# Softmax sums moved from a second exponential to accumulating DMAs and a product with ones, with one-term scores for the maxima and a new order of work

## The reference

```
h = layernorm(x)                                   # over the 512 features, eps 1e-6
shift, scale, gate = split(silu(cond) @ mod_w + mod_b, 3)     # per batch
h = h * (scale + 1) + shift
q, k, v = split(h @ w_qkv)                         # 16 heads of 32 features
q = rope(layernorm(q) * q_norm_w); k = rope(layernorm(k) * k_norm_w)
scores = q @ k.T / sqrt(32)                        # per head, 512 x 512
o = softmax(scores) @ v
out = x + (o @ w_out) * gate
```

## Time and profile before

| what | us |
|---|---|
| runs: median (lowest to highest) | 1943.38 (1943.3 to 1945.53) |
| profiled execution, its own time | 1946.49 |
| span of the profiled execution | 1944.7 |
| TensorE busy | 1776.7 |
| VectorE busy | 1485.0 |
| ScalarE busy | 1487.2 |
| GpSimd busy | 434.4 |

### The profile page before, as it was taken

The page is one execution under the profiler, slowest core; times in us unless marked ns, Lnnn a source line. Parts: engine busy times, 40 slices in busy tenths (PEclk is TensorE's granted clock), DMA queues, the critical chain, the costliest instruction groups (busy, mean ns, idle before and its releaser), DMA issues.

```text
span 1944.7 us, 35999 instructions
## 1 busy us (share of the span) xinstructions
PE 1776.7 (91%) x13346; PEld 1030.4 (53%) x13346; DVE 1485.0 (76%) x2430; ACT 1487.2 (76%) x3145; POOL 434.4 (22%) x452
## 2 busy tenths in 40 slices
PE   4768899999999999999999999999999999997777
PEld 1645555555555555555555555555555555554333
DVE  6677778888888788878887888788878888875443
ACT  2248888888888888888888888888888888887663
POOL 0331222122212221222122212221222122221000
PEclk8879999999999999999999999999999999998769
DMA  5000010100101111010101010010111002000001
GB/s 193 27 6 28 6 44 23 50 28 17 55 28 50 34 39 34 23 55 17 55 28 50 23 49 29 18 55 28 50 33 40 28 17 63 16 28 22 21 18 66
DMA packets 35950, 72.77 MB, mean 37 GB/s; under 512 B 4513, under 2 KB 4513, under 8 KB 35778
## 3 DMA queue, kind: packets, MB, share of 16 engines
q1 hardware_dynamic: 35778, 70.47, 11.3%
HBM read 53.58 MB, written 16.88 MB: 36 GB/s over the span
## 4 chain that ended last, share of the span: by engine, by line
PE 80%; ACT 9%; issue 5%; DVE 5%; DMA 1%; ACTq 0%; SPq 0%; DVEq 0%
PE Y L261 26%; PE SM L370 13%; PE SA L397 10%; PE O L415 10%; PE Y L268 10%; ACT SM L527 4%; PE SA L401 3%; PE O L352 3%; PE SA L252 2%; ACT vals L504 2%; PE SA L379 2%; DVE qk_lo L676 1%; DVE qk_hi L674 1%; ACT probs L542 1%; ACT oT L519 1%
## 5 line engine op out<-in xcount | busy, mean ns | idle before, releaser
L527 ACT ACTIVATE SM<-SM,negmax 128x512 f32<-128x512 f32 x512 | 338.7, 664 | 130.8 <-DVE negmax L683 130.8
L683 DVE TENSOR_REDUCE negmax<-SM 128x2 f32<-128x1024 f32 x256 | 313.6, 1225 | 162.6 <-PE MB L370 155.9
L851 POOL TENSOR_TENSOR pair_part<-rows,rope_pair 128x256 f32<-128x256 f32 x128 | 94.5, 739 | 1312.8 <-DVE rows L660 1307.7
L527 ACT ACTIVATE MB<-MB,negmax 128x512 f32<-128x512 f32 x512 | 341.9, 671 | 0.0
L542 ACT ACTIVATE probs<-SM 128x1024 f32<-128x1024 f32 x256 | 262.8, 1027 | 72.0 <-PE SM L401 54.6
L683 DVE TENSOR_REDUCE negmax<-MB 128x2 f32<-128x1024 f32 x256 | 310.9, 1215 | 0.0
L261 PE MATMUL Y<-wqkv_hi,hT_hi 128*128 128x512 f32 x728 | 307.4, 422 | 0.3 <-ACT rows L493 0.3
L261 PE MATMUL Y<-wqkv_hi,hT_lo 128*128 128x512 f32 x728 | 306.7, 421 | 0.0
L415 PE MATMUL O<-probs,vals 128*32 128x512 f32 x2048 | 283.8, 627 | 5.9 <-ACT probs L543 5.9
L261 PE MATMUL Y<-wqkv_lo,hT_hi 128*128 128x512 f32 x728 | 289.2, 397 | 0.0
L543 ACT ACTIVATE probs<-SA 128x1024 f32<-128x1024 f32 x256 | 260.8, 1019 | 0.0
(11 more groups left out here) (140 smaller groups left out, 4108.6 us busy)
## 6 DMA issues: line engine op xcount, KB each, us to landing
xin<-in_x_dram SPq DMA_DIRECT2D x64, 256.0 KB, 2.9
xres<-in_x_dram SPq DMA_DIRECT2D x60, 256.0 KB, 2.6
out_dram<-xres SPq DMA_DIRECT2D x60, 256.0 KB, 2.0
shift_scale<-mod_rows SPq DMA_DIRECT2D x16, 512.0 KB, 4.2
gate<-mod_rows SPq DMA_DIRECT2D x16, 256.0 KB, 4.7
rows<-in_L_cond_mod_w_dram SPq DMA_DIRECT2D x1, 3072.0 KB, 10.0
probs<-in_L_cond_w_qkv_dram SPq DMA_DIRECT2D x2, 1024.0 KB, 12.7
vals<-in_L_cond_w_qkv_dram SPq DMA_DIRECT2D x1, 1024.0 KB, 15.6
```

Source lines behind the costliest of these rows:

```text
L527: ins = act.activation(qm_bank(i), qm_bank(i), ACT.Exp, bias=negmax[:, g % 2, t, i:i + 1], accum_out=sums[:, g % 2, t, i:i + 1])
L683: dve.tensor_reduce(negmax[:, g % 2, t, 2 * half:2 * half + 2], bank[:], AX.X, ALU.max, negate=True).then_inc(max_out, 1)
L851: pool.tensor_tensor(pair_part[:].rearrange("p h (i two) -> p h i two", two=2), swapped, rope_pair[:, t, j, :].rearrange("p (i two) -> p i ...
```

## The change

- **Scores by query** keep only the hi*hi term; they now serve only to find maxima. The maxima, negated, go straight into `cst`, without a logarithm; the low part that `cst` held is gone.
- **Key exponentials** therefore give unnormalized probabilities, three buffers of them. Their sum over a group's four key blocks is made by GpSimd-issued accumulating DMAs (`add_keys`): block 1 is added onto block 0's buffer, then 2, then 3, each 128 x 2048 float32. A float32 product with ones (`add_over_keys`) sums that buffer over its 128 partitions and spreads it over each head's 32 rows. ScalarE takes the logarithm and the exponential of its negative (`log_sums`, `inverse_sums`), and VectorE multiplies the finished oT by it (`scale_o`). For the last group only blocks 1 and 2 are added by DMA; the product with ones takes two buffers.
- **qk high parts** move from VectorE to ScalarE (`high_qk`); q and k are transposed into MB instead of O, one group ahead instead of two, with two ring buffers instead of three. Squares are taken from SBUF after the copy (`square`).
- **Roots** are guessed by ScalarE (exp(-ln/2), `guess_roots`) with one Newton step: 4 VectorE instructions instead of 11.
- **Order**: a quarter on TensorE is scores by key, values, scores by query, then one whole projection of 12 matmuls; high terms first. v is projected for tile s+4, q for s+6, k for s+5 or s+6; the output projection is of tile s-5. `xin` has two buffers instead of three.
- **Start**: weights come in pieces, w_q first; the modulation runs as four products side by side in four column groups, whose parts are added by a selection product. Batch 0's shift and scale come from that product directly, without DRAM. The first four tiles' statistics and roots are made together; the low parts of w_q and w_v are made by GpSimd; five tiles and their q, k, v products are ordered by hand before the loop.

The core of the diff:

```diff
@@ scores by query
-                for a, c in ((qk_hi, qk_hi), (qk_hi, qk_lo), (qk_lo, qk_hi)):
-                    for i in range(HG):
-                        r = head_rows(i)
-                        mm = pe.matmul(qm_bank(i), a[r, ring, 0, cols], c[r, ring, 1, :],
-                                       start=(a is qk_hi and c is qk_hi), stop=(a is qk_lo))
+                for i in range(HG):
+                    r = head_rows(i)
+                    mm = pe.matmul(qm_bank(i), qk_hi[r, g % 2, 0, cols], qk_hi[r, g % 2, 1, :], start=True, stop=True)
@@ TensorE, new
+            def add_over_keys(g, bank, buffers):
+                for m, a in enumerate(buffers):
+                    for i in range(HG):
+                        mm = pe.matmul(bank[head_rows(i), :], ones_r[:, 0:E].bitcast(F32), probs[:, a, i, :],
+                                       start=(m == 0), stop=(m == len(buffers) - 1), skip_group_check=True)
+                mm.then_inc(ones_done, 1)
@@ TensorE, one step
+            for s in range(LAST + 1):
+                transpose_c(s)
+                if group(s + 1):
+                    transpose_qk(s + 1, 0)
+                    transpose_qk(s + 1, 1)
+                scores_by_key(s, 0)
+                if s > 0:
+                    weigh_values(s - 1, 3)
+                if group(s + 1):
+                    scores_by_query(s + 1, 0)
...
+                    project(s + 4, 2, Y[:])
+
+                scores_by_key(s, 1)
+                if s > 0:
+                    pe.wait_ge(third_added, 16 * s)
...
+                    add_over_keys(s - 1, MB[:, 0, :], (sum_buffer(s - 1),))
+                weigh_values(s, 0)
+                if group(s + 1):
+                    scores_by_query(s + 1, 1)
...
+                    project_out(n, Y[:], 0, 4)
+                if tile(s + 6):
+                    transpose_x(s + 6)
+                if n >= 0:
+                    project_out(n, Y[:], 4, 12)
+
+                scores_by_key(s, 2)
+                weigh_values(s, 1)
+                if group(s + 1):
+                    scores_by_query(s + 1, 2)
...
+                    project(s + 6, 0, Y[:])
...
+                scores_by_key(s, 3)
+                weigh_values(s, 2)
+                if group(s + 1):
+                    scores_by_query(s + 1, 3)
+                if tile(s + 6):
+                    pe.wait_ge(raw_out, raw_count(s + 6, 0))
+                    project(s + 6, 1, Y[:])
@@ ScalarE
-            def query_exponentials(g, t, half):
...
+            def high_qk(g, j):
...
+                act.activation(qk_hi[:, g % 2, j, :], MB[:, j, :], ACT.Copy).then_inc(qk_high, 1)
+            def log_sums(g, bank):
...
+                act.activation(sum_inv[:], bank, ACT.Ln).then_inc(sum_ln, 1)
+            def inverse_sums(g):
+                act.wait_ge(sum_ln, g + 1)
+                act.activation(sum_inv[:], sum_inv[:], ACT.Exp, scale=-1.0).then_inc(sum_ready, 1)
+                    if t == 0:
+                        if g > 0:
+                            act.wait_ge(pv_step, n - 1)
+                            act.wait_ge(second_added, 16 * g)
...
+                    elif t == 1 and g > 0:
+                        act.wait_ge(pv_step, n - 1)
+                        act.wait_ge(third_added, 16 * g)
...
+                    elif t == 3:
+                        act.wait_ge(pv_step, n - 1)
+                        act.wait_ge(first_added, 16 * (g + 1))
@@ VectorE
+            def scale_o(g):
+                o = oT[:, (g // NG) % 2, g % NG, :]
+                dve.wait_ge(sum_ready, g + 1)
+                dve.wait_ge(o_out, g + 1)
+                dve.tensor_tensor(o, o, sum_inv[:], ALU.mult).then_inc(o_scaled, 1)
@@ GpSimd
+            def add_keys(g, t):
+                pool.wait_ge(s_exp, 2 * (TT * g + t) + 2)
+                if t == 1:
+                    pool.wait_ge(pv_step, TT * g + 1)
+                else:
+                    pool.wait_ge((first_added, second_added)[t - 2], 16 * (g + 1))
+                pool.dma_start(probs[:, sum_buffer(g)].rearrange("p h n -> p (h n)"),
+                               probs[:, probs_buffer(g, t)].rearrange("p h n -> p (h n)"), accum_op=ALU.add
+                               ).then_inc((first_added, second_added, third_added)[t - 1], 16)
+            for s in range(LAST + 1):
+                add_keys(s, 1)
+                if s - 5 >= 0:
+                    add_residual(s - 5)
+                if tile(s + 5):
+                    rotate(s + 5, 0)
+                add_keys(s, 2)
+                if tile(s + 5):
+                    rotate(s + 5, 1)
+                if s < LAST:
+                    add_keys(s, 3)
@@ start, SyncE
+            load_weight(0)
+            load_modulation(1)
+            load_modulation(0)
...
+            load_weight(2)
+            load_weight(1)
+            load_modulation(2)
```

More of the change, by code:

```diff
@@ L270, in project_out, with project_last @@
                     mm.then_inc(y_done, 1)
-            def project_last(t, bank, first, last):
+            def project_last(t, first, last):
+                bank = last_banks[t]
                 for g in range(first, last):
-                    for o, w in ((last_hi, wout_hi), (last_hi, wout_lo), (last_lo, wout_hi)):
-                        mm = pe.matmul(bank, o[:, g, t * P:(t + 1) * P], w[:, g, :],
-                                       start=(g == 0 and o is last_hi and w is wout_hi),
-                                       stop=(g == NG - 1 and o is last_lo))
+                    for i, (o, w) in enumerate(((last_hi, wout_hi), (last_hi, wout_lo), (last_lo, wout_hi))):
+                        mm = pe.matmul(bank, o[g][:, t * P:(t + 1) * P], w[:, g, :],
+                                       start=(g == 0 and i == 0), stop=(g == NG - 1 and i == 2))
@@ L461, in _, with modulation_parts @@
-            weigh_values(LAST, TT - 1)
-            pe.wait_ge(s_exp, 2 * TT * NS)
-            project_last(3, last_banks[3], 0, 3)
+            def modulation_parts(j, bank):
+                pe.wait_ge(ld_mod[j], 16)
+                for c in range(DT):
+                    mm = pe.matmul(bank[head_rows(c), :], siluT[:, c, :], modw_raw[j][:, c, :],
+                                   start=True, stop=True, skip_group_check=True)
+                mm.then_inc(mod_partial, 1)
+            pe.wait_ge(siluT_ready, 1)
@@ new lines, in _ @@
+            modulation_parts(1, SM[:, 1, :])
+            modulation_parts(0, SM[:, 0, :])
+            pe.wait_ge(sel_step, 4)
+            for j in (1, 0):
+                pe.wait_ge(parts_out, 2 - j)
+                pe.matmul(MB[:, j, :], sel_first, parts_sb[:, j, :], start=True, stop=True).then_inc(mod_first, 1)
+            for j in (1, 0):
+                pe.matmul(SM[0:NB, j, :], sel, parts_sb[:, j, :], start=True, stop=True).then_inc(mod_product, 1)
+            transpose_x(0)
+            project(0, 0, Y[:])
@@ new lines, in _ @@
+            pe.wait_ge(parts_out, 3)
+            pe.matmul(O[0:NB, :], sel, parts_sb[:, 2, :], start=True, stop=True).then_inc(mod_product, 1)
+            transpose_qk(0, 0)
+            transpose_qk(0, 1)
+            pe.wait_ge(raw_out, raw_count(4, 0))
+            project(4, 1, Y[:])
+            scores_by_query(0, 0)
+            transpose_x(5)
+            pe.wait_ge(raw_out, raw_count(4, 1))
+            project(5, 0, Y[:])
+            scores_by_query(0, 1)
+            pe.wait_ge(raw_out, raw_count(5, 0))
@@ L594, in _ @@
             dve.tensor_tensor(silu_sb, silu_sb, cond_sb, ALU.mult).then_inc(silu_ready, 1)
[L595 to L599 removed]
+            for c in range(1, DT):
+                if c > 1:
+                    dve.wait_ge(sel_step, c - 1)
+                dve.tensor_tensor(sel, ident[:, 0:NB] if c == 1 else sel, ident[:, E * c:E * c + NB], ALU.add
+                                  ).then_inc(sel_step, 1)
@@ new lines, in _ @@
+            weight_mean(0)
+            weight_centre(0)
+            modulation_sum(0, 1, SM[:, 1, :])
+            modulation_sum(1, 0, SM[:, 0, :])
+            for n in range(TT):
+                first_statistics(n)
+            for n in range(TT):
+                aggregate_first(n)
+            first_inverse_roots()
+            normalize_x(0)
+            normalize_x(1)
+            x_low(0)
+            weight_mean(1)
+            x_low(1)
+            weight_centre(1)
+            normalize_x(2)
```

994 lines of the change are left out of this document (576 added, 418 removed).

## The result

The kernel after takes 1991.22 us (median of 4 runs, 1983.11 to 1993.28) against 1943.34 us: ratio 1.0236, 95% interval 1.0205 to 1.0267. It is slower; 1817 us was forecast. The profiled execution took 1993.06 us, its span is 1991.3 us. First the page of the kernel after: busy time, the queue of the accumulating DMAs, the shares of the chain that ended last, and three DMA issues.

The account below looks back on a forecast made before the run. Bound before: TensorE's work (some 26.2 of 27.84 us per group) and a bank's round trip together. Lead in -58, groups 0-4 -5, 53 groups -55, tail -11, close +3: -126 from 1943.4, about 1817 us; 8 in 10: 1735 to 1990.

Parts of the forecast that it names:

- lead in: Time before group 0: forecast to start at about 85 us instead of 142.8, -58 us, between -38 and -68.
- close: After the last group: two chained sums, 16 ones matmuls, logarithm, exponential and multiply, some +3 us, up to +10.
- tail: Groups 58 to 62, without projections and at a lower clock: 28 us each, -11 us, at worst 0.
- Cycle (a): Per-group loop from ones product through projection, normalization and q's rotation to two DMAs: 12.0 + 2D, 26.8 us.
- D: One 1 MB accumulating DMA from issue to landing: 7.4 us taken, bounds 4.0 and 12.0.
- fixed part: Cycle (a) without its DMAs: 9.0 us to normalized rows plus 3.0 for q's rotation, 12.0 us.
- The terms for TensorE: TensorE's dense work of 24.6 us per group plus small waits, 25.7 us if nothing else holds it.
- Cycle (b): Per-group loop of three chained DMAs plus exponentials and logarithm ahead of the first: 3D + 3.4, limiting from 8.6 on.
- (1): Rival: DMAs fast, D up to 6.85, TensorE with small waits sets 25.7 us per group; about 1754 us; chance 0.27.
- (2): Rival: slow accumulate, ones product and exponential wait; break-even 29.0 us per group at D 8.5, about 2200 at 10; chance 0.20.
- (3): Rival: VectorE's order does not fit, maxima late; at +1.5 us per group about 1840 us; chance 0.10.
- (4): Rival: TensorE's pauses lower its clock; 30 us or more per group, about 2000 us; chance 0.05.

Follow-up runs that it names:

- e5: Kernel after with the three-term by-query scores of before put back: 2013.86 us, ratio 1.0354 to the kernel before.
- e2: Kernel after with the second accumulating DMA issued ahead of the rotation of q: 1956.48 us, ratio 1.0080 to the kernel before.
- e3: Kernel after with siluT moved to a free part of gated and GpSimd's wait before the first rotation removed: 1973.58 us, ratio 1.0150 to the kernel before.
- e4: Kernel after with the DMAs copying instead of adding (sums incomplete, good for time alone): 1807.69 us, one run.
- e6: Kernel after with two accumulating DMAs, ones product over two buffers and moved earlier, second DMA ahead of both rotations: 2018.25 us, ratio 1.0377 to before.
- e9: Kernel after with the third add as a GpSimd instruction and the second DMA ahead of q's rotation: 1960.95 us, ratio 1.0073 to the kernel before.
- e11: e6 plus e3's lead in and VectorE's list reordered (last maxima earlier, output parts behind first maxima): 1956.43 us, ratio 1.0064 to the kernel before.
- e12: e9 plus e3's lead in and VectorE's list reordered as in e11: 1845.22 us, ratio 0.9490 to the kernel before.
- e1: Kernel after with each accumulating DMA moving 512 KB instead of 1 MB (sums incomplete, good for time alone): 1826.78 us, one run.
- e7: Kernel after with all three adds as GpSimd instructions instead of DMAs: 2217.18 us, ratio 1.1401 to the kernel before.

## Why the prediction was wrong

The sum missed by 174 us: 1991 for 1817. By stretches: groups 5 to 57, 124 us (29.14 for 26.8); groups 0 to 4, 12; lead in, 31; close, 7; tail, nothing.

**The mechanism of the forecast was right, the size of its cycle wrong.** Cycle (a), "12.0 + 2D" with D = 7.4, gave 26.8 us and is in the chain link by link; it closes in every group from 6 to 57. What it measures there, in the mean:

| term | forecast | measured | difference |
|---|---|---|---|
| fixed part, clock at 2.4 GHz | 12.0 | 12.85 | +0.85 |
| clock at 1.2 GHz in 12 of 52 groups | none | 0.41 | +0.41 |
| other late issues, 3 groups | none | 0.03 | +0.03 |
| issue between second and third add | none | 0.57 | +0.57 |
| second and third add | 14.8 | 8.08 + 7.16 = 15.24 | +0.44 |
| together | 26.8 | 29.10 | +2.30 |

So the step that failed is the fixed part of 12.0 us, which was mis-sized: it is 13.9 us with the clock and the issue between the adds, and that is 1.9 of the 2.3 us; the DMA's duration, called the unknown of the forecast, was nearly right and is 0.4. In the fixed part the roots take 1.8 us instead of 0.9, with the step that stands out GpSimd's residual add, the rotation 3.3 instead of 3.0; ones to projection is 0.4 us shorter. Over groups 5 to 57 (29.14 us) the 2.3 us a group are the 124 us; they turned a gain of 1.04 us a group into a loss of 1.30.

The shortest adds take 6.9 to 7.0 us, as the third does in 41 of the 52 groups and the second in 13; the longest takes 10.1. In the steady stretch of the trace the median is 7.0 us where no other transfer is under way, 7.7 beside two and 8.1 beside three. That is an association; no run moved the loads away.

**The terms for TensorE were nearly right and did not matter.** With cheap DMAs a group takes 26.15 to 26.4 for 25.7. Of the 1.84 us that e5 gives back to TensorE, 0.35 show.

**Cycle (b), "3D + 3.4",** was 0.7 us short: it is 3D + 4.1, of other links than the prediction named (e2). At the median D = 7.7 that gives 27.2 us. But the three adds of a group are not alike: in e2 they take 8.0, 8.6 and 7.2 us in the mean, 23.9 together, which gives 28.0; most of the other 0.5 us of e2's 28.47 is from groups in which the first add goes out later than 3.0 us after the landing (19 of 52).

**The lead in** failed at a step that the prediction did not have. It asked only whether weight splits would delay the rotations; it did not ask which memory `siluT` shared (13.6 of 31 us, e3), and it left out the mean and centring of the k weight ahead of the first projection (5.7 us).

**The close** has the second chained add of 6.9 to 10.1 us, then store, xres and gate loads one behind another (5.0, 6.6 and 4.3 us in the chain); only the sums had been counted.

**The rivals.** (1) is what e4 shows, 1808 for 1754, and falls with D = 7.6. (The 1746 us put beside the estimate of 6.2 us does not follow from the recorded sum: at 6.2 us TensorE sets the group, as in rival (1), and that is 1754.) (2) has the right sign, but by another cycle, at a D below its 8.5 (where, by the forecast's own terms, it is still cycle (a) that sets the group, at 29.0). Its break-even was too kind as well: outside groups 5 to 57 the change gives back 22 us, not 71, so these break even at 28.25 us. (3) is not the limit after, as the maxima (cst L938) have 1% of the chain there; it limits once the chain of adds is shortened (part of e6, most of e9: the new order gives 0.84 us from e6 to e11 and 1.99 from e9 to e12), by ordering and by SBUF operations held up by GpSimd. (4) fell in its size and holds in small: the clock of groups 5 to 57 is 0.98 against 1.00 before, since it drops to 1.2 GHz in 14 short stretches; in twelve groups the drop lies on the ones product and the values, which are links of the cycle, and costs the 0.41 us a group above, 21 us in all.

**The Trainium skill's sentence on VectorE's copies** (SBUF — State Buffer, "SBUF: two separate sides") had been weighed in one direction only, VectorE holding up GpSimd. What this kernel pays for is the other one: GpSimd's instruction running, VectorE's waiting for its end (0.8 us of each group in the one root step: 1.04 us in the mean for 0.20 before).

## What to carry over

Before a reduction moves to DMAs, write down the cycle that its landing closes, with each engine's in-order list between landing and next issue, and give that cycle slack in microseconds rather than in busy share: here a cycle forecast 1.1 us above TensorE's limit came out 3 us above it (29.14 to 26.15), four fifths of the miss in its many small links and not in the DMA. TensorE's links of such a cycle stand right behind its wait for the sum; here they ran at 1.2 GHz in 12 of 52 groups. Split a serial chain of adds over two kinds of engine, and place the maxima that the next group waits for ahead of VectorE's SBUF work (e12). The maxima, which read PSUM, keep their time beside GpSimd; the cast does not, though it has a single input. When a scratch tile is shared at the start, ask which wait that sharing adds.

## What was not expected of the hardware

- Several kinds of VectorE instruction from SBUF to SBUF wait until a running GpSimd instruction ends, whatever their size: 128x33 elements 0.2 to 1.2 us, a 128x512 cast 0.41 to 3.7 us, a 128x512 normalization 0.75 to 4.5 us. The maxima from PSUM kept 1.22 us in all kernels.
- An accumulating DMA within SBUF costs as much as two reads: 1 MB 7.6 us, as a copy 4.8, 512 KB 4.8.
- Beside these adds, 256 KB loads of x take 7.1 us for 2.9 before, 4.7 to 4.8 in e4 and e1, and 2.6 in e7, without the queue. They go with the length of the transfer beside them, not with the queue's share of the DMA engines: with it at 34 to 37% (e6, e9, e11, e12) they still take 7.1 to 7.2 us. In the kernel after 49 of the last 57 loads land 0 to 0.8 us after the add that they run beside.
- TensorE's clock fell to 1.2 GHz in 14 short stretches of groups 5 to 57, in twelve groups right behind a wait for the sum, though the clock of the whole stretch reads 0.98. Before the change it was 1.00 there.
